# Moving work out from between the value product and its denominators in a causal attention kernel

## What is computed

```python
q, k, v = heads(x @ wq), heads(x @ wk), heads(x @ wv)      # 32 query heads, 8 key heads, 32 wide
q, k = rope(q), rope(k)
scores = einsum('bhqd,bkhd->bhqk', q, k) / sqrt(32)        # causal mask
attn = softmax(scores, axis=-1)
out = einsum('bhqk,bkhd->bqhd', attn, v) @ wo
```

## Time and profile before

| what | value |
|---|---|
| median of 3 runs | 3132.68 us (3129.05 to 3140.56) |
| profiled execution, its own time | 3125.46 us |
| its span in the profile | 3123.7 us |
| PE busy | 2780.1 us, 89% of the span |
| DVE busy | 2122.1 us, 68% |
| ACT busy | 1000.7 us, 32% |
| mean granted clock of TensorE | 0.949 of full speed |

### The profile page before, as it was taken

The page is one execution under the profiler, slowest core; times in us unless marked ns, Lnnn a source line. Parts: engine busy times, 40 slices in busy tenths (PEclk is TensorE's granted clock), DMA queues, the critical chain, the costliest instruction groups (busy, mean ns, idle before and its releaser), DMA issues. The chain is left out here.

```text
span 3123.7 us, 48871 instructions
## 1 busy us (share of the span) xinstructions
PE 2780.1 (89%) x15824; PEld 1787.1 (57%) x15824; DVE 2122.1 (68%) x4647; ACT 1000.7 (32%) x1549; POOL 302.1 (10%) x403
## 2 busy tenths in 40 slices
PE   7899998999999799752868999989999996997999
PEld 6555454654554488652646555546554542886887
DVE  7777787777787433588777878777778784324543
ACT  2234344134343411352521434442234344101000
POOL 2011111010111000000020111110010110001111
PEclk9999999999999899865979999999999998998999
DMA  4323121323131422000133323123223121433111
GB/s 157 94 63 97 53 82 62 113 73 97 53 99 36 140 81 67 0 0 0 81 135 99 97 59 99 53 79 119 70 66 93 54 81 69 161 133 149 68 67 41
DMA packets 121071, 252.90 MB, mean 81 GB/s; under 512 B 12720, under 2 KB 39728, under 8 KB 120880
## 3 DMA queue, kind: packets, MB, share of 16 engines
q1 hardware_dynamic: 120912, 251.03, 25.5%
HBM read 166.57 MB, written 84.41 MB: 80 GB/s over the span
## 5 line engine op out<-in xcount | busy, mean ns | idle before, releaser
L505 ACT ACTIVATE a_prob<-a_pst 128x1024 f32<-128x1024 f32 (+3 forms) x768 | 593.4, 816 | 728.1 <-PE a_pst L796 727.0
L605 DVE CUSTOM_DVE_ANT_0 a_psh<-a_psh,a_edge 128x128 f32<-128x128 f32 (+3 forms) x1024 | 487.0, 513 | 154.4 <-PE a_psh L749 146.4
L749 PE MATMUL a_psh<-a_kst,a_qst 127*128 127x512 f32 (+3 forms) x1536 | 515.3, 396 | 41.0 <-DVE a_mx L605 20.4
L749 PEld LDWEIGHTS a_psh<-a_kst,a_qst 127*128 127x128 f32 x1536 | 256.6, 189 | 472.0 <-DVE a_mx L605 222.2
L796 PE MATMUL a_pst<-a_qst,a_kst 128*128 128x512 f32 (+2 forms) x1536 | 399.8, 361 | 28.4 <-ACT a_prob L505 10.4
L608 DVE TENSOR_REDUCE a_mx<-a_psh 128x1 f32<-128x512 f32 x512 | 343.7, 689 | 72.5 <-PE a_psh L749 65.8
L816 PE MATMUL a_ppv<-a_prob,a_vg 128*32 128x512 f32 (+3 forms) x3072 | 333.3, 506 | 13.6 <-POOL a_prob L435 11.6
L796 PEld LDWEIGHTS a_pst<-a_qst,a_kst 128*128 128x128 f32 x1536 | 268.1, 193 | 125.6 <-issue 53.0
L816 PE MATMUL a_pden<-a_prob,a_ones 128*32 128x512 f32 (+3 forms) x3072 | 328.4, 499 | 0.0
L435 POOL TENSOR_SCALAR_AFFINE_SELECT a_prob<-a_prob 128x512 f32<-128x512 f32 x256 | 179.1, 700 | 1304.0 <-ACT a_prob L505 1304.0
L652 DVE RECIPROCAL a_dens<-a_dens 128x512 f32<-128x512 f32 x64 | 214.6, 3353 | 67.8 <-ACT a_dens L513 55.5
(11 more groups left out here) (214 smaller groups left out, 3812.6 us busy)
## 6 DMA issues: line engine op xcount, KB each, us to landing
a_qst<-q SPq DMA_DIRECT2D x192, 256.0 KB, 4.5
a_wraw<-in_wqkv SPq DMA_DIRECT2D x52, 512.0 KB, 5.8
q<-a_stg_hi SPq DMA_DIRECT2D x64, 256.0 KB, 3.1
q<-a_stg_lo SPq DMA_DIRECT2D x64, 256.0 KB, 3.3
oT<-a_oT SPq DMA_DIRECT2D x64, 256.0 KB, 2.5
a_kst<-kT SPq DMA_DIRECT2D x96, 128.0 KB, 3.0
h_oraw<-oT SPq DMA_DIRECT2D x16, 512.0 KB, 4.0
h_x<-in_x SPq DMA_DIRECT2D x16, 512.0 KB, 4.7
```

Source lines behind the costliest of these rows:

```text
L505: act.activation(prob[k % 2][:, 2 * half:2 * half + 2, off:], pst[:, half, :, off:], ACT.Exp, scale=scale).then_inc(s["exp_done"], 1)
L605: part = dve.tensor_tensor_reduce(scores, scores, edge[:, BANK - n:], 1.0, 2 * MASKED, ALU.add, ALU.max, mx_hq[kc][:, h, qt:qt + 1])
L749: mm = pe.matmul(psh[:, at, i * n:(i + 1) * n], qst[par][0:P - 1, h, qt * P:(qt + 1) * P], kst[par][0:P - 1, kc * BANK:kc * BANK + n], sta ...
```

## The change

```diff
+TOGETHER = (0, 1, 2, 3, 9, 10, 11)
 
 def iteration(full_s=True, proj=True, ahead=False):
...
         total, done, k = sum(map(columns, window)), 0, 0
+        slot = {("PV", e, 0): ("ST", e + 1, 1) for e in TOGETHER}
         for step in window:
             done += columns(step)
             while k < len(USES) and k * total < done * len(USES) - total // 2:
-                after[step] += [("S", k)]
+                after[slot.get(step, step)] += [("S", k)]
                 k += 1
...
     order = [("ST", 0, 0), ("ST", 0, 1)] + ([("HI", 1), ("LO", 1), ("RS", 1)] if full_s else []) + first
+    for e in TOGETHER:
+        after["PV", e, 1][:0] = after["PV", e, 0]
+        after["PV", e, 0] = []
     for unit in steps:
         for step in unit:
             order += [step] + after[step]
```

## The result

| | before | after |
|---|---|---|
| median of 11 runs each | 3132.25 us (3122.70 to 3140.56) | 3147.83 us (3142.68 to 3152.42) |
| profiled execution, its own time | 3125.46 us | 3150.72 us |
| its span | 3123.7 us | 3149.0 us |
| mean granted clock | 0.949 | 0.947 |

The ratio is 1.0053, with a 95% interval of 1.0040 to 1.0065: the changed kernel is slower by 15.6 us, between the medians. The two profiled executions differ by more (25.3 us), because before's is one of its faster ones and after's one of its slower ones.

The account below looks back on a forecast made before the run. PE was taken to bound the kernel, with DVE level or behind at units 0 to 2. Groups +14.2 us and clock +2.4 made +16.6, so 3149 us for the median against 3132.7; range 3118 to 3168.

Parts of the forecast that it names:

- Price of a pair of switches, 0.33: PE going between full-width and 32-wide matmuls and back: 0.33 us per unit whose parts come together, 134 x 0.33 = 44 us.
- What bounds units 0 to 2: At each group's start DVE is level with PE or behind: odd-group waits of 0.7 at S1 and S2, 0.3 at S4.
- Odd groups, +0.67: Second group of each loop turn, 12 in all: +0.47 unit 0, +0.13 unit 2, +0.40 unit 9, -0.33 unit 10.
- so 0.47 of the 0.86 come through: Odd groups, unit 0: the projection ends 0.86 us later, but DVE was busy anyway, so `rotate` starts only 0.47 later.
- S2 follows `rotate` by 3.97 us: Odd groups: a DVE chain of `rotate` and S0's maximum sets S2, so S2 moves from 409.64 to 410.11.
- Even groups, +0.20: First group of each loop turn, 8 counted: S2 unmoved, then 0+0.13+0.40-0.33; waits become 2.2 at S1 and 0.6 at S2.
- First groups, +0.76: First group of each batch entry, 4 in all, where DVE had waited 2.84 us for the projection: +0.76 us each.
- the mean of 0.56: First groups, unit 0: up to 0.86 us of projection delay comes through, less in two of four; 0.56 taken on average.
- The clock, +2.4: Two more even groups fall to 1.2 GHz behind their waits, about 1.2 us each; bounds none to 20 us.
- full-width work stays covered: Rival, chance 0.12: with banks free early enough, all 134 pairs pay, 3089 us; half of it about 3110.
- A wash: Rival, chance 0.14: waits of S4, S35 and S36 at half the price, 3142 us or a little under.
- The clock falls in most groups: Rival, chance 0.13: new waits in odd and even groups drop PE to 1.2 GHz in most of them, 3167 us.

Follow-up runs that it names:

- the small mask: The changed kernel, with POOL blanking only 4 of the 128 columns of each head in unit 2: 3144.94 us in one execution, odd groups 54.21 us.
- unit 0 alone: Against the kernel before, only unit 0's two parts brought together, its last two P pieces behind the denominators: 3152.28 us, ratio 1.0062.
- unit 9 alone: Against the kernel before, only unit 9's two parts brought together, with S35 and S36 ahead of them: 3147.98 us, ratio 1.0052.
- units 1 and 2 alone: Against the kernel before, only the parts of units 1 and 2 brought together, with S1 and S4 ahead of them: 3130.28 against 3130.73 us, ratio 1.0003.
- unit 10 alone: Against the kernel before, only unit 10's two parts brought together (24 body and 2 ahead7 groups): 3121.64 against 3133.06 us, ratio 0.9966.

## Why the prediction was right

The forecast was 3149 us, and 3147.8 came. The mechanism is the one that was forecast; several sizes are not. Step by step:

- **Price of a pair of switches, 0.33.** Right in odd groups, where it is read best: +0.32 when unit 3 is drawn apart, -0.38 when unit 10 is brought together. The latter is a little more than 0.33, and that difference was not looked into.
- **What bounds units 0 to 2.** Right in kind: `rotate` in odd groups is ended by PE, S1 waits for the shuffle's bank, S2 and S4 for maxima. The prediction had 0.7, 0.7 and 0.3 for their waits; they are 0.56, 0.91 and 0.17.
- **Odd groups, +0.67.** Too low; +0.80 was measured. The term that was mis-sized is unit 0, "so 0.47 of the 0.86 come through": with the waits it is 0.74. The step that failed is "S2 follows `rotate` by 3.97 us". It follows it by 4.23 (191.11 to 195.34), because the sum takes 0.27 longer beside POOL's mask; the small mask takes 0.26 of the 0.80 away again. Units 1 and 2 were +0.13 and measured +0.08, unit 9 +0.40 and +0.37 (S35 0.24 late instead of 0.25, S36 with 0.17 of waiting instead of 0.3), unit 10 -0.33 and -0.38.
- **Even groups, +0.20.** Too high; +0.06 was measured. The +0.13 for unit 2 is there: from S2 to S15 it is 11.64 us, before 11.53. Units 9 and 10 cancel instead of leaving 0.07: the product with cos behind unit 10 starts 28.58 us behind S15 in the mean, and 28.59 before. The rest is within what even groups differ among themselves. The waits came out as worked out: 2.08 at S1 (2.2) and 0.63 at S2 (0.6).
- **First groups, +0.76.** Too low. Units 0 to 2, from the first ST of a batch entry to S15, went from 24.29 to 25.38 us where the clock held in both profiles (first entry of the second layer), and from 25.74 to 26.98 where it fell in both (second entry of the first): +1.09 and +1.24, where the prediction had 0.56 and 0.13. The run with unit 0 alone gives +1.12. The mis-sized term is the mean of 0.56. In the second layer's first entry DVE waits 3.37 us for the projection instead of 2.51, so the whole 0.86 comes through, and the sum of `rotate` takes 0.96 here too. The other two first groups can't be compared, since the clock fell in one of the two profiles only.
- **The sum.** 12 x 0.80, 8 x 0.06, 4 x 1.17 and 4 x 0.37 for `body6`, whose unit 9 I price from the run with unit 9 alone, are 9.6+0.5+4.7+1.5 = 16.3 us, where the prediction had 14.2. What else changes in `body6` and `ahead7` was not measured by itself. The medians differ by 15.6 us, 12.5 to 20.4 by the interval, so the groups alone can give all of it.
- **The clock, +2.4.** Nothing shows it. The mean granted clock of the eleven executions of the changed kernel is 0.9477, and that of the kernel before is 0.9469, 0.9475 and 0.9479 in the three rounds of experiments. Nor can a profile tell: the stretches of the attention stages that fell to 1.2 GHz number 7 in before's first profile, 14 in its second and 13 in after's, and of the eight even groups they met three, five and four. A fall was also cheaper than the 1.2 us that the prediction took. In the four even groups of the changed kernel it cost 0.3 to 0.9 us, since it came behind the long wait at S1 and slowed the two parts ahead of S2, behind which PE would have waited 0.63 in any case. So that 3149 was met to some 1 us is in part luck: the groups were put 2 us too low, and the term of the clock made up for it.

With unit 9 alone and unit 0 alone the clock does seem to count. Their medians lie 4.5 and 5.9 us above what their groups add up to. Their executions have a mean granted clock of 0.9444 and 0.9438, against 0.9469 for the kernel before in the same round, and among the 22 executions of the latter 0.001 of clock goes with 1.5 us. That makes an estimate of 3.8 and 4.7 us. In their profiles the clock falls in four of the eight even groups each, and for longer than in the changed kernel, which costs 2.1 to 2.6 us each. Why it falls so in these versions and not with the whole change was not looked into; with units 1 and 2 alone it fell in none, in one profile.

The rival "full-width work stays covered" gets its case from unit 10 alone, and fails everywhere else for the reason that was given against it. "A wash" is out by the interval. "The clock falls in most groups" is out: no odd group of the changed kernel's profile is longer than 54.52.

The waits that killed the gain are read in the maxima's rows, but what makes DVE late at S2 is its own list ahead of it, `rotate` and the four maxima of S0. The Trainium skill, TensorEngine Tiling, PSUM Bottleneck, says that tiling doesn't speed up the emptying of PSUM. In this kernel's terms that is what the rows show, at S1, S2, S4 and S36, with waits of 0.56, 0.91, 0.17 and 0.17 us in an odd group.

## What to carry to other kernels

Price a switch of shape in the program itself, at a place where the two parts already stand together, and then ask of every step that moves past them which buffer it waits for there. Work between two parts is not only a cost: it was the time in which the other engine emptied a bank, and packing producers against two banks hands the saving to the waits. Bring together only where the step in between waits for nothing (unit 10: 11 us), and judge each place by itself, as the places of this change came to +0.74 (unit 0), +0.08 (units 1 and 2), +0.37 (unit 9) and -0.38 us (unit 10) in an odd group.

## What the runs showed of the hardware

A DVE sum of two SBUF operands takes 0.69 us alone and 0.96 us when POOL's mask of 128x512 starts before it. In the kernel before the sum started first (407.88), and the mask paid instead, 1.12 us where it takes 0.64 to 0.69 alone. The Trainium skill, SBUF — State Buffer, Who interferes with whom, says that a DVE instruction with two SBUF inputs and a GpSimd instruction that reads SBUF contend, since the second input comes through a read interface that the two share. It also says: "Issue order, not op shape, decides who blocks." This case agrees: in the kernel before the sum was ahead of the mask by 0.08 us and kept its 0.69; in the changed kernel the mask was there first and the sum paid 0.27. Even the mask of 16 columns took 0.73 us: it started 0.05 behind the product with sin (187.99 and 187.94), which also has two inputs in SBUF, and ended 0.09 behind it. Nothing of the change touches POOL; it only brought the mask forward against `rotate`.

The granted clock of the same program at the same place was 1.00 in one execution and 0.50 in another, behind the same two waits of PE. A single profile of such a place is no evidence for what a change does to the clock.
